# A recommendation tower on one core: the pair stage written out by chunk, moved by DMA, with paced gathers

## The chip, the cores and the metric

The kernel runs on one core of one Trainium2 chip. The metric is the device time of one execution in microseconds. A core has TensorE (PE: matmuls, with its weight loads shown apart as PEld), VectorE (DVE), ScalarE (ACT), GpSimd (POOL) and SyncE (SP), which run their own instruction streams in order and meet at semaphores. In a trace an fp32 matmul shows as two weight loads and two matmul records; a transpose shows as one of each. The documents below call one such weight load with its matmul a pass.

## The reference, cut to what matters

For 512 samples, 26 embedding rows of 64 numbers each are gathered from 26 tables. Then, with fixed weights:

```python
x = layer_norm(dense_t @ Wd.T, gd, bd)                       # 512 x 128
y = layer_norm(einsum('bnd,ed->bne', sparse_t, Ws), gs, bs)  # 26 rows of 128 per sample
y = layer_norm(einsum('bne,pn->bep', y, Wsi), gsi, bsi)      # 32 columns of 128 per sample
T = concatenate([x, y])                                      # 33 vectors of 128 per sample
Z = einsum('bnd,bmd->bnm', T, T)                             # all pair products
out = layer_norm(Z[lower triangle] @ Wl.T, gl, bl)[first 384 live]
h = relu(concatenate([out, dense]) @ W_top1 + b_top1)
h = relu(h @ W_top2 + b_top2);  y = h @ W_top3               # 512 x 1
```

## The kernel before, in words

The 512 samples are taken in NG = 4 granules of GRAN = 128, and a granule in NC = 4 chunks of 32 samples. A granule's 26 rows of 128 samples fill 13 tiles of two rows side by side (tile `G`), 4 tiles for chunk 0 and 3 for each other chunk. POOL gathers them with one indirect DMA for each tile and side: 8 for chunk 0, 6 for each other chunk, 26 a granule, 104 in all (L285). `G` holds one granule, so the gathers of a chunk wait until the chunk in the same place of the granule ahead was read by TensorE (`ut_ps`). Nothing else holds the gathers back.

One chunk goes through these steps. TensorE transposes the gathered tiles (`transpose_rows`, L941), multiplies them by a Gram matrix (`gram_rows`, L947), DVE turns that into a variance (`variance1`, L673, L677), ACT takes a root and DVE scales the rows (`scale_rows`, L683, L686). TensorE sums the fields into 32 columns a sample (`project_fields`, L958) and embeds them (`embed`, L968); DVE moves them to `V` (`y_evacuate`, L696), ACT squares them (`square2`, L381), DVE sums the squares (`variance2`, L701), ACT takes the root (L385), and DVE scales `V` (`normalise2`, L705, L707).

The pair products (`pair_products`, L990) run on half a granule, 64 samples: one matmul for each sample, weights 128x32 and 34 moving columns (32 of `V`, one of x, one of ones). Four samples stand beside one another in four column groups of 32. Of the symmetric products a ring of 16 columns is kept: `z_evacuate` (ACT, L390) copies the first 16 columns, `z_merge` (DVE, L748, L749) overwrites by a mask with the other 16. When a granule is done, `spread_pairs` (TensorE, L1002, L1008) brings them into blocks of 128 pairs by samples with 24 matmuls against pieces of the unit matrix, and ACT copies them to `zb` and `zx` (`z_copy`, L397, L398).

`project_pairs` (L1022) makes the 512 features of the granule, with features on partitions: 4 feature blocks by 5 pair blocks, 20 matmuls 128 columns wide. `f_squares` (L402), `sum_blocks3` (DVE, L712), `sum_squares` (TensorE, L1030), `deviation3` (ACT) and `normalise3` (DVE, L716, L718) normalise them. `layer1` (L1045), `layer2` (L1054), `layer3` (L1062) follow.

The order is written by hand for each engine. A granule's 4 slots are `slots01` and `slots23`; the work on pairs of a granule is spread over the slots of the granules behind it. Slots of the middle granules are in a hardware loop (`Fori(1, NG - 1)`, two passes) on ACT, DVE and TensorE (L552, L863, L1196); the first and last are written out. SP has the weight loads at the start, each behind the landing of a chunk of gathers of granule 0 (L258 to L266), and the one store at the end.

## Time and profile before

| what | value |
|---|---|
| time, median of 3 runs | 244.02 us (243.06 to 245.71) |
| profiled execution, its own time | 243.04 us |
| its span | 241.2 us, 4708 instructions |
| PE busy | 173.7 us (72%), 1983 passes |
| PEld busy | 131.6 us (55%) |
| DVE busy | 121.1 us (50%), 225 instructions |
| ACT busy | 76.2 us (32%) |
| POOL busy | 108.1 us (45%), 104.0 of it gathers |
| mean granted TensorE clock | 0.83 of full |
| "issue" on the chain of waits | 17% of the span |
| "another core or an unknown queue" on it | 13% |
| DMA traffic | 8.14 MB, mean 34 GB/s |

The span runs from the first to the last instruction; the execution's own time is 1.8 us more. Busy times are of one engine and overlap with those of others. "issue" is time in which an engine waited for nothing that the profile shows. "remote" stands where the profile knows no releaser. The two levels of the granted clock are 1.2 and 2.4 GHz; a fraction is a mean over them.

### The profile page before, as it was taken

How to read it: one execution, taken by the hardware profiler on the slowest of the kernel's cores; microseconds unless marked ns; L12 is line 12 of the kernel's file. 1: busy time of each engine (PE TensorE's matmuls, PEld its weight loads, DVE VectorE, ACT ScalarE, POOL GpSimd, SP SyncE). 2: the span in 40 equal slices, each digit the busy share in tenths (PEclk: the TensorE clock that was granted, in tenths of full speed). 3: DMA queues.
4: the chain of work that ended last, by engine and by line, in shares of the span. 5: the costliest groups of instructions: out<-in, count | busy, mean ns of one | idle time of the engine just before them, and what ended most of it. 6: DMA issues, size and time to landing. Idle time of an engine off the chain costs nothing.

```text
span 241.2 us, 4708 instructions
## 1 busy us (share of the span) xinstructions
PE 173.7 (72%) x1983; PEld 131.6 (55%) x1983; DVE 121.1 (50%) x225; ACT 76.2 (32%) x158; POOL 108.1 (45%) x110
## 2 busy tenths in 40 slices
PE   0668825649981954689558728979929799867896
PEld 0318721235551724458528518846729686767695
DVE  6474400238958270546482920916863984773012
ACT  2021400026684420515321310414414165350224
POOL 3787777727775173456570660557450000330000
PEclk9985555757996796899875955997967999999999
DMA  6515453101111010010110010011010000000000
GB/s 190 178 24 125 111 155 97 45 5 26 28 22 29 3 30 16 14 22 16 20 26 8 16 24 6 11 24 22 16 27 0 0 0 1 0 3 5 0 3 0
DMA packets 5728, 8.14 MB, mean 34 GB/s; under 512 B 2357, under 2 KB 3279, under 8 KB 5712
## 3 DMA queue, kind: packets, MB, share of 16 engines
q0 software_dynamic: 3328, 3.41, 7.4%
q1 hardware_dynamic: 1664, 3.65, 5.0%
q10 hardware_dynamic: 720, 0.85, 1.2%
q8 instruction: 12, 0.20, 0.4%
q14 instruction: 4, 0.03, 0.0%
HBM read 7.91 MB, written 0.00 MB: 33 GB/s over the span
## 4 chain that ended last, share of the span: by engine, by line
PE 53%; issue 17%; another core or an unknown queue 13%; DVE 9%; ACT 5%; DMA 2%; ACTq 1%; DVEq 0%
PE ps_z L990 8%; PE ps_gq L947 6%; PE ps_y L968 5%; PE ps_ut L958 5%; PE ps_tail L1045 4%; PE ps_tail L1022 3%; PE ps_z L1002 3%; PE ps_tail L899 2%; DVE var L701 2%; DMA gs_sb<-in_gs_row_dram 2%; PE ps_y L1022 2%; PE ps_gq L941 2%; PE ps_tail L931 2%; PE ps_tail L1054 1%
## 5 line engine op out<-in xcount | busy, mean ns | idle before, releaser
L285 POOL DMA_INDIRECT G<-in_table_dram,idx x104 | 104.0, 1000 | 74.9 <-PE ps_ut L958 41.7
L990 PE MATMUL ps_z<-V 128*32 128x34 f32 x1024 | 21.1, 218 | 28.0 <-issue 26.3
L673 DVE TENSOR_TENSOR qg<-ps_gq,G 128x384 f32<-128x384 f32 (+1 forms) x16 | 9.4, 588 | 57.0 <-PE ps_gq L947 23.2
L990 PEld LDWEIGHTS ps_z<-V 128*32 128x32 f32 x1024 | 16.9, 128 | 35.3 <-issue 32.3
L968 PE MATMUL ps_y<-ut,wcg 64*128 64x512 f32 x64 | 21.6, 751 | 7.2 <-issue 7.0
L958 PE MATMUL ps_ut<-S,G 128*128 128x192 f32 (+4 forms) x128 | 25.1, 348 | 2.2 <-DVE G L686 1.5
L947 PE MATMUL ps_gq<-gram,gt 128*128 128x128 f32 x104 | 19.2, 335 | 8.9 <-ACT gt L367 7.7
L958 PEld LDWEIGHTS ps_ut<-S,G 128*128 128x128 f32 x128 | 23.5, 229 | 3.2 <-DVE G L686 2.1
L701 DVE TENSOR_REDUCE var<-sq 128x32 f32<-128x1024 f32 x16 | 19.4, 1213 | 8.5 <-ACT sq L381 7.9
L381 ACT ACTIVATE sq<-V 128x1024 f32<-128x1024 f32 x16 | 16.9, 1058 | 20.3 <-DVE V L696 20.3
L947 PEld LDWEIGHTS ps_gq<-gram,gt 128*128 128x128 f32 x104 | 16.4, 236 | 10.5 <-ACT gt L367 7.8
L696 DVE TENSOR_TENSOR V<-ps_y,bias_y 128x512 f32<-128x512 f32 x32 | 20.6, 683 | 2.5 <-remote 2.5
L291 POOL TENSOR_TENSOR V<-V,r_pool 128x1024 f32<-128x1024 f32 x2 | 3.8, 1924 | 31.2 <-DVE r_pool L817 31.2
L707 DVE TENSOR_TENSOR V<-V,r 128x1024 f32<-128x1024 f32 x14 | 17.2, 1226 | 0.5
L367 ACT COPY gt<-ps_gq 128x384 f32<-128x384 f32 (+1 forms) x16 | 8.0, 502 | 29.1 <-PE ps_gq L941 23.7
L1022 PEld LDWEIGHTS ps_tail<-zb,wl 128*128 128x128 f32 x96 | 13.3, 214 | 3.9 <-issue 3.8
L1022 PE MATMUL ps_tail<-zb,wl 128*128 (+1 forms) x96 | 15.1, 307 | 0.0
L372 ACT ACTIVATE sd<-var,eps 128x6 f32<-128x6 f32 (+1 forms) x16 | 4.8, 300 | 29.1 <-DVE var L677 22.5
L941 PE MATMUL ps_gq<-eye,G 128*128 128x128 f32 x52 | 10.8, 332 | 3.6 <-issue 2.0
L376 ACT COPY ut<-ps_ut 128x512 f32<-128x512 f32 x16 | 9.4, 586 | 12.2 <-remote 8.0
L1045 PE MATMUL ps_tail<-zn,w1z 128*128 128x128 f32 x72 | 10.5, 308 | 2.5 <-DVE zn L718 1.2
L1045 PEld LDWEIGHTS ps_tail<-zn,w1z 128*128 128x128 f32 x72 | 9.9, 221 | 2.8 <-issue 2.6
(138 smaller groups left out, 228.3 us busy)
## 6 DMA issues: line engine op xcount, KB each, us to landing
G<-in_table_dram,idx POOLq DMA_INDIRECT x104
w1z<-in_w_z_dram SPq DMA_DIRECT2D x1, 768.0 KB
wl<-in_wl_blocks_dram SPq DMA_DIRECT2D x1, 768.0 KB
dns<-in_dense_t_dram ACTq DMA_DIRECT2D x1, 512.0 KB
w1d<-in_w_d_dram SPq DMA_DIRECT2D x1, 512.0 KB
wl<-in_wl_blocks_dram SPq DMA_DIRECT2D x1, 512.0 KB
w2s<-in_w_dram SPq DMA_DIRECT2D x1, 512.0 KB
wrow<-in_wsi_rows_dram SPq DMA_DIRECT2D x1, 208.0 KB
```

The lines of the kernel that those rows point to most:

```text
L285: pool.indirect_dma_start(G[:, j, g, :], None, table, bass.IndirectOffsetOnAxis(ap=idx[:, k:k + 1], axis=0)).then_inc(gathered[c], 16)
L381: act.activation(sq2[:, :, :], chunk_v(c), ACT.Square).then_inc(sq_ready, 1)
L696: dve.tensor_tensor(V[:, b0:b0 + CB, 0:NPROJ], ps_y[:, g, :].rearrange("p (b q) -> p b q", q=NPROJ), bias_y[:, :].unsqueeze(1).broadcast_t ...
L701: dve.reduce_sum(var2[:, :], sq2[:, :, :], AX_X).then_inc(var2_ready, 1)
L707: dve.tensor_tensor(chunk_v(c), chunk_v(c), r2[:, :].unsqueeze(2).broadcast_to([P, CHUNK, NPROJ]), ALU.mult).then_inc(v_ready, 1)
L941: mm = pe.transpose(ps_gq[:, n * P:(n + 1) * P], G[:, j, :, :].rearrange("p g d -> p (g d)"), eye[:, :])
L947: mm = pe.matmul(ps_gq[:, n * P:(n + 1) * P], gt[:, n * P:(n + 1) * P], gram[:, :], start=True, stop=True)
L958: mm = pe.matmul(ps_ut[:, chunk % 2, col:col + n], G[:, j, :, :].rearrange("p g d -> p (g d)"), S[:, j, :, :].rearrange("p s q -> p (s q)" ...
L968: pe.matmul(ps_y[:, g, :], wcg[64 * g:64 * g + 64, :], ut[64 * g:64 * g + 64, :], start=True, stop=True).then_inc(y_ps, 1)
L990: mm = pe.matmul(ps_z[32 * qb:32 * qb + 32, bb // 8, col:col + SLOTS], V[:, b, 0:NPROJ], V[:, b, :], start=True, stop=True)
L1022: mm = pe.matmul(bank[:, lc, :], wl[:, k, lc * P:(lc + 1) * P], rhs, start=(k == 0), stop=(k == KB - 1))
L1045: mm = pe.matmul(tail[:, oc, :], w1z[:, k, oc * P:(oc + 1) * P], zn[:, k, :], start=(k == 0), stop=(k == LLIVE - 1))
```

## The change

- **Gathers.** `G` holds all four granules. The wait for `ut_ps` is gone. Before the gathers of chunk n (n counts all 16 chunks) POOL waits until those of chunk n - 1 have landed. Each chunk has a semaphore of its own.
- **Pair products.** They run by chunk, 16 times, two samples a matmul: weights 128x64 (two samples' 32 columns), 67 moving columns (one of ones, two of x, 64 of `V`), two matmuls beside one another in two column groups of 64. 16 matmuls a chunk, 256 in all, for 512. Of each result the two samples' own blocks are used.
- **Evacuation.** `z_evacuate` is two ACT copies a chunk; `z_merge` two COPY_PREDICATED and two small copies on DVE a chunk. The places of the samples are permuted in the gathers' ids so that they come out in order.
- **Moves.** For granules 0 to 2 `spread_pairs` and `z_copy` go. SP issues 24 DMAs a granule from `zt` to `zb` and `zx`, 32 partitions each, rows of 128 bytes. Granule 3 keeps the matmuls (`last_spread`).
- **Projection.** For granules 0 to 2 samples are on partitions: 5 matmuls, 512 columns wide, for 20 of 128. The squares are summed by the accumulator of ACT's Square, root and scale are one number a partition (ACT does the scale), three transposes turn the features back (`transpose_features`), ACT copies them to `zn`. `sum_blocks3`, `sum_squares` and `normalise3` go.
- **Order.** All loops are written out. Slot n has `transpose_rows(n)`, `project_fields(n-1)`, `gram_rows(n)`, `embed(n-1)`, `pair_products(n-2)`, and the evacuation of chunk n-3. In the last granule POOL scales one chunk of `V`, for two before.
- **Start.** `prepare_b1`, `prepare_x` and the dense products are placed later or one by one through `ps_tail`.

```diff
-        G = sb("G", [P, TILES, 2, D])
+        G = sb("G", [P, NG, TILES, 2, D])
...
-            for gp in range(NG):
-                for c in range(NC):
-                    if gp:
-                        pool.wait_ge(ut_ps, nth(gp - 1, c))
-                    for j in batch(c):
-                        for g in range(2):
-                            k = gp * 2 * TILES + 2 * j + g
-                            pool.indirect_dma_start(
-                                G[:, j, g, :], None, table,
-                                bass.IndirectOffsetOnAxis(ap=idx[:, k:k + 1], axis=0)).then_inc(gathered[c], 16)
-            for n, c in enumerate(POOL_CHUNKS):
-                pool.wait_ge(r2_ready, nth(NG - 1, c))
-                pool.tensor_tensor(chunk_v(c), chunk_v(c), r2_pool[:, n, :].unsqueeze(2).broadcast_to([P, CHUNK, NPROJ]),
-                                   ALU.mult).then_inc(v_pool_ready, 1)
+            for n in range(NCHUNK):
+                if n > 0:
+                    pool.wait_ge(gathered[(n - 1) // NC][(n - 1) % NC], 2 * len(batch((n - 1) % NC)) * 16)
+                for j in batch(n % NC):
+                    for g in range(2):
+                        k = n // NC * 2 * TILES + 2 * j + g
+                        pool.indirect_dma_start(
+                            G[:, n // NC, j, g, :], None, table,
+                            bass.IndirectOffsetOnAxis(ap=idx[:, k:k + 1], axis=0)).then_inc(gathered[n // NC][n % NC], 16)
...
+            def move_pairs(gp):
+                sp.wait_ge(z_merged, (gp + 1) * NC)
+                for qb in range(4):
+                    src = zt[32 * qb:32 * qb + 32, gp % 2, :, qb % 2, :]
+                    at = slice(gp * GRAN + 32 * qb, gp * GRAN + 32 * qb + 32)
+                    for q in range(4):
+                        sp.dma_start(zb[32 * q:32 * q + 32, :, at], src[:, PQ * q:PQ * q + PQ, :]).then_inc(z_moved, 16)
+                    sp.dma_start(zx[ROW_XV:ROW_XV + 32, at], src[:, RING, :]).then_inc(z_moved, 16)
+                    sp.dma_start(zx[ROW_S:ROW_S + 32, at], src[:, RING + 1, :]).then_inc(z_moved, 16)
+            for gp in range(NG - 1):
+                move_pairs(gp)
...
+            def z_evacuate(n):
+                if n >= 2 * NC:
+                    act.wait_ge(z_moved, (n // NC - 1) * MOVES * 16)
+                act.wait_ge(z_ps, n + 1)
+                for w in range(2):
+                    last = act.copy(z_places(n, w), z_pairs(w)[:, :, :, 0:RING])
+                last.then_inc(z_first, 1)
...
+            def f_squares(gp):
+                act.activation(f_sq[:, :, :], tail, ACT.Square, accum_out=f_sum[:, :]).then_inc(f_sq_ready, 1)
+            def deviation3(gp):
+                act.wait_ge(f_sq_ready, gp + 1)
+                act.activation(sd3[:, 0:1], f_sum[:, :], ACT.Sqrt, bias=eps[:, :], scale=1.0 / L).then_inc(sd3_ready, 1)
+            def f_scale(gp):
+                act.wait_ge(r3_ready, gp + 1)
+                act.activation(f_scaled[:, :, :], tail[:, 0:LLIVE, :], ACT.Copy, scale=r3[:, 0:1]).then_inc(f_ready, 1)
+            def zn_copy(gp):
+                act.wait_ge(ft_ps, gp + 1)
+                act.copy(zn[:, :, :], tail[:, 0:LLIVE, :]).then_inc(zn_ready, 1)
...
+            def z_merge(n):
+                dve.wait_ge(z_first, n + 1)
+                for w in range(2):
+                    dve.copy_predicated(z_places(n, w), mmask[:, :].unsqueeze(1).unsqueeze(1).broadcast_to([P, 4, 2, RING]),
+                                        z_pairs(w)[:, :, :, RING:NPROJ])
+                x_at, s_at = (zt[:, n // NC % 2, m, :, n % NC * 8:n % NC * 8 + 8].rearrange("p l (w s) -> p w s l", w=2)
+                              for m in (RING, RING + 1))
+                dve.tensor_copy(x_at, z_slots[:, :, :, 1:3])
+                dve.tensor_copy(s_at, z_slots[:, :, :, 0:1].broadcast_to([P, 2, 4, 2])).then_inc(z_merged, 1)
...
+            def slot(n):
+                gp, c = divmod(n, NC)
+                normalise2(n - 2)
+                if n >= 3:
+                    z_merge(n - 3)
+                if c == 1 and gp > 1:
+                    add_dense(gp - 2)
+                variance1(n)
+                x_slots(n - 1)
+                scale_rows(n)
+                if n == 3:
+                    prepare_last_block()
+                if c == 3 and gp > 0:
+                    root3(gp - 1)
+                y_evacuate(n - 1)
+                variance2(n - 1)
...
-                for bb in range(16):
-                    for qb in range(4):
-                        b = h * HALF + 16 * qb + bb
-                        col = (bb % 8) * SLOTS
-                        mm = pe.matmul(ps_z[32 * qb:32 * qb + 32, bb // 8, col:col + SLOTS], V[:, b, 0:NPROJ],
-                                       V[:, b, :], start=True, stop=True)
+                    pe.wait_ge(z_merged, n)
+                for w in range(2):
+                    for s in range(4):
+                        for ct in range(2):
+                            v = n % NC * CB + 8 * w + 2 * s + ct
+                            mm = pe.matmul(ps_z[64 * ct:64 * ct + 64, w, s * SLOTS:(s + 1) * SLOTS], V[:, v, 3:SLOTS],
+                                           V[:, v, :], start=True, stop=True)
                 mm.then_inc(z_ps, 1)
...
+            def project_pairs(gp):
+                pe.wait_ge(wl_ready, 2)
+                pe.wait_ge(dense_ready, OC1)
+                if gp > 0:
+                    pe.wait_ge(yo_ready, gp)
+                pe.wait_ge(z_moved, (gp + 1) * MOVES * 16)
+                at = slice(gp * GRAN, (gp + 1) * GRAN)
+                for k in range(KB):
+                    mm = pe.matmul(ps_tail[:, :], zb[:, k, at] if k < PB else zx[:, at], wl[:, k, :],
+                                   start=(k == 0), stop=(k == KB - 1))
+                mm.then_inc(f_ps, 1)
...
+            def slot(n):
+                gp, c = divmod(n, NC)
+                transpose_rows(n)
+                project_fields(n - 1)
+                gram_rows(n)
+                if n == 3:
+                    prepare_dense(1)
+                if n == 4:
                     prepare_last_block()
+                if n == 5:
+                    prepare_dense(2)
+                if n == 6:
+                    prepare_dense(3)
+                if c == 3 and gp > 0:
+                    project_pairs(gp - 1)
+                if c == 0 and gp > 1:
+                    transpose_features(gp - 2)
+                if c == 1 and gp > 1:
+                    layer2(gp - 2)
+                embed(n - 1)
+                pair_products(n - 2)
+                if c == 0 and gp > 1:
+                    layer1(gp - 2)
+                if c == 1 and gp > 1:
+                    layer3(gp - 2)
...
+            gp, n = NG - 1, NCHUNK - 1
+            transpose_rows(n)
+            project_fields(n - 1)
+            gram_rows(n)
+            embed(n - 1)
+            pair_products(n - 2)
+            project_fields(n)
+            embed(n)
+            project_pairs(gp - 1)
+            pair_products(n - 1)
+            transpose_features(gp - 1)
+            pair_products(n)
+            layer1(gp - 1)
+            last_spread(gp)
+            layer2(gp - 1, ocs=range(1))
+            last_project_pairs(gp)
+            last_layer1(gp, range(1))
+            last_sum_squares(gp)
+            last_layer1(gp, range(1, OC1))
+            layer2(gp - 1, ocs=range(1, OC2))
+            last_layer2(gp)
+            layer3(gp - 1)
+            last_layer3(gp)
...
```

## Rows read from the trace of the kernel before

**Rows 1.** The longest waits of the whole span: engine, line, releaser, total, times, longest.
```profile
...
PE ps_z L990 <- issue: 26.3, 34, 1.8
...
```

**Rows 2.** The gathers, all shapes: busy, mean ns, idle before, releasers.
```profile
...
L285 POOL DMA_INDIRECT G<-in_table_dram,idx x104 | 104.0, 1000 | 74.9 <-PE ps_ut L958 41.7 <-issue 28.0 <-DVE idx L570 3.2
...
```

**Rows 3.** Stretches with gathers in flight, then one without: width, busy (records) by engine.
```profile
...
71.60:78.60 7.00, 1.21 (x12) 0.78 (x12) 4.87 (x8) 2.63 (x5) 3.95 (x5) 0.72 0.13 25
87.00:94.40 7.40, 1.59 (x20) 1.17 (x19) 2.05 (x5) 0.23 (x1) 4.69 (x5) 0.82 0.16 29
...
136.70:145.40 8.70, 2.53 (x26) 1.50 (x27) 3.36 (x7) 1.25 (x2) 5.73 (x6) 0.67 0.15 26
...
188.30:189.70 1.40, 1.32 (x129) 1.19 (x128) 1.36 (x3) 0.67 (x2) 0.00 (x0) 1.00 0.00 0
...
```

**Rows 4.** The same view, from a gather burst's start until the pair products stall.
```profile
...
118.81:123.50 4.69, 4.28 (x51) 2.72 (x51) 2.19 (x4) 1.28 (x4) 3.78 (x4) 0.64 0.13 24
134.02:136.70 2.68, 2.54 (x50) 1.36 (x48) 2.58 (x5) 1.21 (x4) 2.07 (x3) 1.00 0.07 12
172.12:174.50 2.38, 2.36 (x54) 1.37 (x53) 1.52 (x3) 0.68 (x3) 1.89 (x2) 1.00 0.07 14
...
```

**Rows 5.** Time line of POOL: start, length, operation, idle before.
```profile
...
21.93 0.95 POOL L285 DMA_INDIRECT G<-in_table_dram,idx  x1 [0.30 <-issue]
...
91.96 0.95 POOL L285 DMA_INDIRECT G<-in_table_dram,idx  x1 [0.30 <-issue]
...
118.81 0.95 POOL L285 DMA_INDIRECT G<-in_table_dram,idx  x1 [1.59 <-remote]
...
```

**Rows 6.** Time line of TensorE, four wide passes and the end of a stalled burst.
```profile
...
84.49 1.98 PE L915 MATMUL ps_tail<-dns,w1d 128*128 128x512 f32 x4
...
94.47 1.24 PE L990 MATMUL ps_z<-V 128*32 128x34 f32 x67 [0.49 <-issue]
...
```

**Rows 7.** Time line of SyncE's DMA issues.
```profile
...
16.86 0.33 SPq L259 DMA_DIRECT2D pmask<-in_pair_mask_dram  x1
...
17.70 0.43 SPq L261 DMA_DIRECT2D w1d<-in_w_d_dram  x1
24.27 8.18 SPq L264 DMA_DIRECT2D wl<-in_wl_blocks_dram  x2
...
```

**Rows 8.** DMA issues: size, median us from issue to landing.
```profile
...
wd<-in_wd_t_dram ACTq DMA_DIRECT2D x1, 128.0 KB, 2.3
...
```

**Rows 9.** Groups by line and shape, DVE and ACT: count, busy, mean ns.
```profile
...
L701 DVE TENSOR_REDUCE var<-sq 128x32 f32<-128x1024 f32 x16 | 19.4, 1213 | 8.5 <-ACT sq L381 7.9 <-issue 0.6
...
L707 DVE TENSOR_TENSOR V<-V,r 128x1024 f32<-128x1024 f32 x14 | 17.2, 1226 | 0.5
L381 ACT ACTIVATE sq<-V 128x1024 f32<-128x1024 f32 x16 | 16.9, 1058 | 20.3 <-DVE V L696 20.3
...
L673 DVE TENSOR_TENSOR qg<-ps_gq,G 128x384 f32<-128x384 f32 x12 | 6.6, 553 | 45.8 <-remote 19.5 <-PE ps_gq L947 19.2 <-issue 7.0
...
L705 DVE RECIPROCAL r<-sd 128x32 f32<-128x32 f32 x14 | 4.8, 344 | 0.4 <-ACT sd L385 0.4
...
L749 DVE COPY_PREDICATED zt<-mmask,ps_z 128x256 f32<-128x256 int32 x8 | 3.8, 470 | 0.0
...
L748 DVE COPY zt<-ps_z 128x32 f32<-128x32 f32 x8 | 1.5, 186 | 5.1 <-ACT zt L390 5.1
...
```

**Rows 10.** Time line of DVE, first chunks.
```profile
...
46.60 0.56 DVE L673 TENSOR_TENSOR qg<-ps_gq,G 128x384 f32<-128x384 f32 x1 [19.52 <-remote]
...
56.11 0.56 DVE L673 TENSOR_TENSOR qg<-ps_gq,G 128x384 f32<-128x384 f32 x1 [0.85 <-PE ps_gq L947]
...
```

**Rows 11.** Time line of DVE, last granule.
```profile
...
191.41 1.28 DVE L696 TENSOR_TENSOR V<-ps_y,bias_y 128x512 f32<-128x512 f32 x2
...
203.88 0.56 DVE L673 TENSOR_TENSOR qg<-ps_gq,G 128x384 f32<-128x384 f32 x1 [3.25 <-PE ps_gq L947]
...
```

**Rows 12.** Time line of ACT at the second pass of the loop.
```profile
...
161.80 0.59 ACT L397 COPY zb<-ps_z 128x512 f32 x1 [6.20 <-remote]
...
```

765 lines of the change are left out of this document (300 added, 465 removed).

## The prediction, made before the changed kernel ran

> **What bounds the kernel now.** I read the waits by total first. The longest of TensorE is on the pair products, with no releaser: 26.3 us in 34 pieces [rows 1]. Then I cut the span around those pieces. In three stretches of 7 to 9 us inside a burst of pair products only 12, 20 and 26 passes ran; in a stretch without the stall 129 ran in 1.40 us [rows 3]. All three lie where POOL issues gathers. One burst resumes at 94.47 [rows 6], 1.56 us after the last gather of its batch left POOL (91.96 + 0.95) [rows 5], and 1.4 us is what a gather takes to land: chunk 1's last one leaves POOL at 22.88 and SP, which waits for it, issues at 24.27 [rows 5, 7]. So the stall ends when no gather is in flight.
>
> The reader is to see a reserve that drains. From the start of a gather burst to the stall TensorE ran 51 passes in 4.7 us, 50 in 2.7 and 54 in 2.4 [rows 4]; in the stall it gets 58 passes in 23.1 us, 2.5 a us [rows 3]. 51 - 2.5 x 4.7 = 39, 50 - 7 = 43, 54 - 6 = 48. I read: TensorE has some 44 passes of instructions in hand, and while gathers fly it is supplied with about 2.5 a us. The trace shows the rates; that it is instruction supply is my inference.
>
> Three other stalls have no releaser: 19.52 us on DVE at the start, ending at 46.60 [rows 10], 6.20 us on ACT at the second pass of the loop [rows 12], and smaller ones. Gathers wait 41.7 us for TensorE [rows 2], but they run ahead and cost nothing by themselves.
>
> **The change, part by part.**
>
> *Gathers.* One takes 1.000 us and 0.30 between two (28.0 over 92) [rows 2], so 104 take 135. Each of 15 pauses costs the landing, 1.4 us, and about 0.1 of handing over: 22. From 3.7 on, the last leaves POOL at 161 and lands at 162.6. Chunks land every 9.2 us, 11.8 for chunk 0. No end of this kernel can be earlier than the last landing, some 3 us to its variance, and the tail.
>
> What a pause gives: after the one of 1.59 us at 118.81 [rows 5] TensorE again had a reserve of 39 [rows 4], though a burst of gathers had only just ended. So I let each pause refill it. Bounds: nothing, and 44 passes plus what runs meanwhile.
>
> *Pair products.* 64 passes a chunk become 32. Four abreast with 34 columns, a pass costs 1.32/129 = 10 ns [rows 3]; with 67 columns and two abreast it is four times that, 41 ns, so 1.3 us a chunk for 0.7. The lower bound is 0.35 us (the rate of before for 32 passes), the upper 32 x 0.5 us = 16 by the pass of 512 columns, far away and taken for nothing. It lies beside DVE.
>
> *Passes.* A slot now needs 53 (3 transposes, 6 Gram, 8 projection, 4 embedding, 32 pairs), chunk 0 three more; the wide projection adds 10 in slots 7 and 11, transposes and layer 1 27 in slots 8 and 12, layers 2 and 3 20 in slots 9 and 13, the start 28. From slot 2 to 14 this is 840.
>
> *DVE in a slot.* Reciprocal 0.34, scaling of V 1.23, variance 0.55 and 0.55, scaling of rows 0.55, sum of squares 1.21 [rows 9], two evacuations 1.28 [rows 11], x column and small reciprocal 0.4. The new z_merge: two COPY_PREDICATED of 128 elements, between half of 0.47 and all of it, I take 0.30 (the halves are strided in four dimensions), and two copies of 0.19 [rows 9]: 1.0, bounds 0.85 and 1.3. Sum 7.1. It waits for ACT's square, 1.06 and 0.1 [rows 9], and about 0.7 for the two roots: 9.0 us a slot. This is a closed chain, since slot n+1 begins with what slot n ends with, so it sets the pace where PE keeps up. ACT's extra copies are hidden in it. The f-path leaves DVE (reciprocal of 128, sum, scaling, 2.6 us a granule), which the 9.0 already leaves out.
>
> *Start.* DVE's stall up to 46.60 [rows 10] stays by my forecast: the same loads follow the same landings. `variance1(2)` then begins at about 56.1 as before [rows 10]. The later places of `prepare_b1` and `prepare_x` are hidden under this stall; without it they would cost under 2 us.
>
> *Moves.* For each granule 24 issues on SP, 0.42 us each (16.86 to 17.70 for two) [rows 7], 10.1, and 2.3 to land [rows 8]: 12.4 us. SP has nothing else queued; the store comes last. z_merge ends 2.6 us into slot n; the projection is wanted before `embed` in slot n+1, which DVE wants 5.0 us into that slot. So the moves are there 12.4 + 2.6 - 9.0 = 6.0 into it. Then come 10 wide passes (four took 1.98 [rows 6], so 4.6) and 1.1 of embedding: 11.7. DVE, and ACT's square behind it, wait 6.7 us, in slots 7 and 11: 13.4. In the last granule the projection stands behind the last `embed`, with 13 us to spare. Bounds of this term: 0 if the passes of the projection fall into a slot that is late anyway, 25 if issues of 128-byte rows take twice as long.
>
> The Trainium skill, DMA: Bandwidth & Descriptors, under "Anatomy of one DMA — SWDGE (gpsimd) path", gives about 2.0 us of fixed cost for a DMA, mostly its completion. As an estimate by that page the 15 pauses would cost 9 us more and the last landing be at 172, still ahead of DVE's pace; the row's 1.4 stands.
>
> *Loops written out.* The stalls at the loop's turn (6.20 on ACT [rows 12]) go. What they hid is next late: DVE's chain. The streams become longer; bounds 0 and one such stall a granule, 18 us.
>
> *Tail.* `variance1` of the last chunk begins at 203.88 [rows 11], 37.3 before the end of 241.2. The last burst is 32 passes, not 128, layer 1 has no reciprocal ahead of it: 35.0. One chunk of V more is scaled by DVE, in the shadow of PE.
>
> *Sum.* 56.1 + 13 slots x 9.0 = 173.1; dmat's eleven small operations 2.1; moves 13.4: 188.6. Supply: from 46.6 to 161.6 it gives 115 x 2.5 = 287 and the 44 in hand, and 44 for each of 11 pauses. By 161.6 slots 2 to 11 must be done, some 630 passes: 7 of 11 refills do, so no cost. 188.6 + 35.0 = 223.6 of span, 225.4 with the 1.8 around it, against 243.0 of the profiled execution. The median of the runs is 1.0 above that; I say 226.
>
> **Rivals.**
>
> *The supply stays starved: slower.* Place: TensorE, slots 2 to 14; price 44 passes, 18 us, for each pause that does not refill, beyond the spare ones. The moves are DMAs too and may fill pauses. To be no slower than before, `variance1(15)` must begin by 207; then slots up to 9 must be done at 161.6, 515 passes: fewer than 5 refills of 11 make it slower. With 4, 331 + 176 passes reach the end of slot 9; 5.1 slots and one wait for moves follow, 161.6 + 46 + 7 + 35 + 1.8 = 251; with none 272. For it: in all bursts the stall begins within a few us. Against it: the pause at 118.81.
>
> The Trainium skill, Runtime: NRT & Kernel Launch, "Instruction fetch mechanics", says that fetch is hidden by the rate of issue and only a taken branch breaks it. By that rule this rival has no ground, and the 26 us would have another cause; the rows at the loop's turn agree with its second half, the stall in unbranched bursts speaks against its first. I give the rival 17 in 100.
>
> *The start-up stall goes, the moves are hidden: the gathers bound.* 162.6 + 3 + 35.0 + 1.8 = 202. For it: the pauses open the same gap for DVE that they open for TensorE. Against: the weight loads are the same bytes. 20 in 100.
>
> *Longer streams stall by themselves.* One stall of 6.2 a granule for three granules, 18 us on top of 226: 244, no change. For it: DVE's 19.52 us is in code without a branch. 11 in 100.
>
> **How the numbers follow.** My case has 52 in 100, by itself 212 to 240 (moves 0 to 25 with 14 taken, z_merge +-3, a wait or two for supply). What a measurement of this kernel can tell from no change is about 1%, 241.6 to 246.5. Slower by over 1%: the starved rival and a little of the stalls, 0.19. Within 1%: most of the third rival's 11, less what lies to its sides, 0.07. Faster: the rest, 0.74. The range is 202 to 246: it holds my case, the gather bound and the third rival, and leaves out the starved one.
>
> **What would show it.** POOL's gathers in 16 groups with about 1.6 us between, the last near 161. Pair bursts of 32 passes without gaps of over a us beside gathers; gaps of 0.7 and 1.2 us there prove the starved rival. DVE's `variance1` every 9 us, with 6 to 7 more in slots 7 and 11, where TensorE waits for the moves. A DVE start near 46; near 32 it is the second rival. I am wrong if DVE idles for long on PE in other slots, if the pause does not refill, or if the moves take far over 12 us.

## The result

The changed kernel takes 264.42 us (median of 4 runs, 259.58 to 266.46), the kernel before 244.87 beside it (243.06 to 246.26): ratio 1.068, interval [1.050, 1.087]. It is slower by 20 us; the forecast was 226. Ratios here and below leave out runs over 1.5% above the fastest of their kernel (here two of the four), so they can differ from those of the medians shown. The profiled execution took 265.47 us, its span is 263.7.

| what | value after |
|---|---|
| PE busy | 176.8 us, 1234 passes |
| PEld, DVE, ACT busy | 124.2, 136.5, 79.8 us |
| POOL busy | 108.7 us |
| mean granted clock | 0.81 |
| on the chain of waits | PE 30%, DVE 20%, issue 14%, ACT 13%, SP's queue 11% |

749 passes fewer, and PE is as busy as before. The longest waits of the kernel after (columns: engine, line, what it waited for, total us, times, longest); the first answers to [rows 1]:

```profile
PE ps_gq L892 <- ACT gt L372: 29.1, 12, 4.6
ACT sq L386 <- DVE V L693: 29.1, 15, 6.8
...
POOL G L290 <- DMA G<-in_table_dram,idx: 24.6, 14, 1.9
...
PE ps_tail L947 <- DMA zx<-zt: 16.3, 3, 8.8
```

TensorE's wait without a releaser on the pair products is no longer among PE's long ones. In its place PE waits for ACT's copy of the transposes, and for the moves. DVE in the kernel after, around its third `variance1` and in one bare slot (start, us, engine, line, operation, what ended the idle time before it); the first line answers to [rows 10], the others to [rows 9]:

```profile
31.48 0.56 DVE L666 TENSOR_TENSOR qg<-ps_gq,G 128x384 f32<-128x384 f32 x1 [5.93 <-issue]
...
45.00 0.56 DVE L666 TENSOR_TENSOR qg<-ps_gq,G 128x384 f32<-128x384 f32 x1 [0.46 <-PE ps_gq L892]
```

```profile
158.71 1.27 DVE L718 COPY_PREDICATED zt<-mmask,ps_z 128x128 f32<-128x128 int32 x2
159.60 0.40 DVE L722 COPY zt<-ps_z 128x16 f32<-128x16 f32 x1
159.67 0.36 DVE L723 COPY zt<-ps_z 128x16 f32<-128x16 f32 x1
159.74 0.67 DVE L666 TENSOR_TENSOR qg<-ps_gq,G 128x384 f32<-128x384 f32 x1
...
162.07 1.28 DVE L693 TENSOR_TENSOR V<-ps_y,bias_y 128x512 f32<-128x512 f32 x2
164.47 1.22 DVE L700 TENSOR_REDUCE var<-sq 128x32 f32<-128x1024 f32 x1 [1.12 <-ACT sq L386]
166.08 0.35 DVE L704 RECIPROCAL r<-sd 128x32 f32<-128x32 f32 x1 [0.39 <-ACT sd L390]
...
168.64 0.67 DVE L666 TENSOR_TENSOR qg<-ps_gq,G 128x384 f32<-128x384 f32 x1
```

The start is 11 us earlier than I took it, since DVE's stall of 19.5 us did not come back (5.9 at 31.48). A slot runs here from one `variance1` to the next, and a bare one is one without preparation, projection or layers; it takes 168.64 - 159.74 = 8.9 us, as worked out. But few are bare. `variance1` begins, for chunks 2 to 15, at 45.00, 58.50, 71.19, 86.84, 98.96, 111.27, 133.80, 149.20, 159.74, 168.64, 192.14, 202.19, 214.38 and 223.28: 13 slots take 178.3 us, for 132.5 forecast.

The moves and the projection of granule 1, on SP's queue and on PE, and the last gather and a pause on POOL, answer to [rows 7, 6, 5]:

```profile
160.06 2.58 SPq L268 DMA_DIRECT2D zb<-zt  x4
162.67 0.61 SPq L269 DMA_DIRECT2D zx<-zt  x1
...
175.00 0.59 SPq L270 DMA_DIRECT2D zx<-zt  x1
```

```profile
176.91 6.64 PE L947 MATMUL ps_tail<-wl,zb 128*128 128x512 f32 x8 [8.80 <-DMA zx<-zt]
183.38 1.02 PE L947 MATMUL ps_tail<-wl,zx 128*128 128x512 f32 x2
184.34 1.13 PE L914 MATMUL ps_y<-ut,wcg 64*128 64x512 f32 x4
```

```profile
17.89 0.94 POOL L290 DMA_INDIRECT G<-in_table_dram,idx  x1 [1.73 <-DMA G<-in_table_dram,idx]
...
162.41 0.95 POOL L290 DMA_INDIRECT G<-in_table_dram,idx  x1 [0.30 <-issue]
```

24 issues take 175.59 - 160.06 = 15.5 us, 0.65 each, and the last has landed 1.3 us after its end. PE waits 8.80 us for them, and then the ten wide passes take 7.4 us, ahead of `embed`. Their granted clock, PE having been idle for 8.8 us, is 0.58 over 177 to 184, mostly the level of 1.2 GHz:

```profile
177.00:184.00 7.00, 7.00 (x10) 2.76 (x10) 0.00 (x0) 0.00 (x0) 0.00 (x0) 0.58 0.00 0
```

(Columns: stretch, length, busy us and number of instructions of PE, PEld, DVE, ACT and POOL, granted clock, DMA share, GB/s.)

In one longer stretch PE does starve, in the pair products of chunk 6 and layer 1 behind them:

```profile
131.78 0.84 PE L933 MATMUL ps_z<-V 128*64 128x67 f32 x21
...
133.78 0.32 PE L933 MATMUL ps_z<-V 128*64 128x67 f32 x3 [0.50 <-issue]
...
136.65 0.49 PE L933 MATMUL ps_z<-V 128*64 128x67 f32 x3 [0.97 <-ACT zn L415]
137.39 4.68 PE L962 MATMUL ps_tail<-zn,w1z 128*128 128x128 f32 x20 [0.25 <-issue]
```

### The profile page after: what moved, and what is told of

It is laid out like the page before. It is cut to its first block, busy times and chain, and to the rows that moved or that the text cites. A ratio compares the mean times of both kernels' runs of the same rounds, so it can differ in the third digit from the quotient of the medians.

```text
span 263.7 us, 3259 instructions
## 1 busy us (share of the span) xinstructions
PE 176.8 (67%) x1234; PEld 124.2 (47%) x1234; DVE 136.5 (52%) x277; ACT 79.8 (30%) x182; POOL 108.7 (41%) x109
## 4 chain that ended last, share of the span: by engine, by line
PE 30%; DVE 20%; issue 14%; ACT 13%; SPq 11%; POOL 5%; DMA 3%; another core or an unknown queue 3%; DVEq 0%
SPq L268 7%; POOL G L290 5%; PE ps_tail L947 5%; DVE V L693 4%; ACT sq L386 4%; DVE var L700 4%; PE ps_tail L962 3%; DVE zt L718 3%; PE ps_y L914 3%; PE ps_tail L971 3%; DVE V L706 3%; PE ps_gq L892 2%; PE ps_ut L904 2%; PE ps_tail L876 2%
## 5 line engine op out<-in xcount | busy, mean ns | idle before, releaser
L290 POOL DMA_INDIRECT G<-in_table_dram,idx x104 | 106.5, 1024 | 56.4 <-issue 28.5
L892 PE MATMUL ps_gq<-gram,gt 128*128 128x128 f32 x104 | 23.4, 387 | 34.8 <-ACT gt L372 29.1
L892 PEld LDWEIGHTS ps_gq<-gram,gt 128*128 128x128 f32 x104 | 19.7, 279 | 37.8 <-ACT gt L372 30.3
L296 POOL TENSOR_TENSOR V<-V,r_pool 128x1024 f32<-128x1024 f32 x1 | 1.9, 1912 | 66.2 <-DVE r_pool L712 66.2
L718 DVE COPY_PREDICATED zt<-mmask,ps_z 128x128 f32<-128x128 int32 x32 | 20.4, 824 | 16.8 <-ACT zt L398 16.8
L700 DVE TENSOR_REDUCE var<-sq 128x32 f32<-128x1024 f32 x16 | 19.5, 1219 | 16.1 <-ACT sq L386 11.7
L933 PEld LDWEIGHTS ps_z<-V 128*64 128x64 f32 x512 | 18.6, 147 | 18.7 <-issue 18.7
L947 PE MATMUL ps_tail<-wl,zb 128*128 128x512 f32 x24 | 16.3, 841 | 16.3 <-DMA zx<-zt 16.3
L933 PE MATMUL ps_z<-V 128*64 128x67 f32 x512 | 21.9, 237 | 5.7 <-DVE zt L723 2.6
L947 PEld LDWEIGHTS ps_tail<-wl,zb 128*128 128x128 f32 x24 | 6.3, 275 | 25.0 <-issue 25.0
L666 DVE TENSOR_TENSOR qg<-ps_gq,G 128x384 f32<-128x384 f32 (+1 forms) x16 | 10.1, 631 | 13.5 <-issue 9.9
L727 DVE RECIPROCAL r<-sd 128x1 f32<-128x1 f32 x3 | 0.5, 164 | 29.5 <-ACT sd L407 18.3
L962 PE MATMUL ps_tail<-zn,w1z 128*128 128x128 f32 x72 | 12.1, 335 | 2.4 <-issue 1.6
```

The lines of the kernel that those rows point to most:

```text
L290: pool.indirect_dma_start(G[:, n // NC, j, g, :], None, table, bass.IndirectOffsetOnAxis(ap=idx[:, k:k + 1], axis=0)).then_inc(gathered[n ...
L700: dve.reduce_sum(var2[:, :], sq2[:, :, :], AX_X).then_inc(var2_ready, 1)
L718: dve.copy_predicated(z_places(n, w), mmask[:, :].unsqueeze(1).unsqueeze(1).broadcast_to([P, 4, 2, RING]), z_pairs(w)[:, :, :, RING:NPROJ])
L892: mm = pe.matmul(ps_gq[:, i * P:(i + 1) * P], gt[:, i * P:(i + 1) * P], gram[:, :], start=True, stop=True)
L933: mm = pe.matmul(ps_z[64 * ct:64 * ct + 64, w, s * SLOTS:(s + 1) * SLOTS], V[:, v, 3:SLOTS], V[:, v, :], start=True, stop=True)
L947: mm = pe.matmul(ps_tail[:, :], zb[:, k, at] if k < PB else zx[:, at], wl[:, k, :], start=(k == 0), stop=(k == KB - 1))
```

## The experiments

**They ran in six sets, and the sets were of two kinds.** Every set carries runs of the kernel before. In the sets of e1 to e4, e9 to e12 and e17 to e18 it took 188.5, 187.8 and 188.3 us; in those of e5 to e8, e13 to e14 and e15 to e16 it took 243.3, 243.3 and 244.8, as in the result. I call them quiet and starved sets. One chip number had a starved set and, later, a quiet one, so it is not a property of the number. Runs are compared within a kind alone.

*The kernel before, unchanged, in a starved and in a quiet set.*

> The kernel before, unchanged. Beside the last four kernels it took 188.5 us, not 244. What makes the difference of 55 us is open. Theory of the supply: the stalls without a releaser are another amount in these runs; the 26.3 us on TensorE's pair products, the 19.5 us on DVE at the start and the 6.2 us on ACT at the loop's turn are below 5 together, and what is left is busy time and the gathers, which then end near 141 (104 x 1.30 + 3.7). Rival, the engines or the transfers themselves were slower then: the mean durations of a gather, of a matmul pass and of DVE's operations are lower here by a like share.

> The kernel before, unchanged, for its profile beside the next three. It took 188 us beside the first four kernels and 243 beside the second four, where the stalls without a releaser were as in the profile shown. If it takes 188 here: no stall without a releaser over 2 us on any engine, the last gather out near 141, the last variance1 near 150, a tail of 37: bound by the gathers. If it takes 243: the stalls are there, and all of them lie before the last gather has landed.

Measured: 241.01 and 187.58 us. Waits in the starved one (e5), then in the quiet one (e9), and the chain of waits of e9 by engine:

```profile
PE ps_z L990 <- issue: 23.4, 43, 1.2
...
DVE qg L673 <- issue: 16.7, 1, 16.7
ACT sd L372 <- issue: 15.5, 5, 8.3
```

```profile
PE ps_z L990 <- issue: 2.2, 2, 1.3
```

```profile
PE 150.8 (81%) x1983; PEld 115.4 (62%) x1983; DVE 120.7 (65%) x225; ACT 75.8 (41%) x158; POOL 111.0 (60%) x110
...
POOL 50%; PE 22%; issue 16%; DVE 7%; ACT 2%; DMA 1%
```

DVE has no such wait in e9 and ACT one of 2.1 us, and PE's on the pair products falls from 23.4 to 2.2. All waits with "issue" or "remote" behind them come to 31, 28 and 50 us on PE, DVE and ACT in e5, and to 3, 0 and 2 in e9. A gather's mean on POOL is 1.03 us in both, and the gathers' packets took 7.4% of 239.2 us in e5 and 10.2% of 185.7 in e9, so the transfers are not quicker. Without the stalls the kernel before is bound by its gathers: the last leaves POOL at 141.06, `variance1` of the last chunk begins at 148.69, and the end is 37.0 later, as expected. What differs from set to set is the waits for nothing that the profile shows; I call them stalls of supply, without knowing what is supplied. With what follows from them they are worth 239.2 - 185.7 = 53.5 us to the kernel before. For the rival (slower engines) speaks only PE: its mean granted clock is 0.84 against 0.95 and its busy time 174.2 us against 150.8. How much of the 53.5 goes through the clock is not separated. DVE's busy time is the same, 121.2 and 120.7 us.

**The traces of the two kinds also differ in how complete they are.** A gather's landing should leave 16 records of a semaphore, 104 x 16 = 1664 in all, as in e1 and e10. The ten traces of quiet sets have 1634 to 1664 of them, the ten of starved sets 262 to 857 (`before` 545, `after` 761, e14 below 262); and their pages give no time from issue to landing for the gathers, where the quiet ones give 2.5 us. Two things follow. In a starved trace the named releasers are uncertain, and an "issue" or "remote" can hide an ordinary wait. And a rival stands that no run tests: that writing the profiler's own records is what holds the engines back in these sets. Every run on record has a span and a clock, so none shows the time without such records.

*The changed kernel, unchanged, in either kind.*

> The changed kernel, unchanged, beside the same runs of the kernel before as the experiments. Late projection took 225.3 us there and the changed kernel without the moves 231.8. Theory of the moves: this is 12 to 15 us above the late projection, 237 to 241, a ratio of 1.26 to 1.28. Rival, the late projection gains nothing: 224 to 228. Variance1 every 9 us, save slots 7 and 11 of 20 to 23 us.

> The changed kernel, unchanged. Theory of two costs: its own chain (slots of 10 to 11 us of DVE, ACT and TensorE by turns, and the moves) makes some 238 us wherever there are no stalls of supply, and the stalls add 25. So if the kernel before takes 188 beside it, this takes 236 to 241; if the kernel before takes 243, this takes 262 to 266. Rival, its time is all supply: then it is below 225 where the kernel before takes 188.

Measured: 263.38 us in the starved set, ratio 1.086 [1.078, 1.095]; 250.99 in the quiet one, ratio 1.337 [1.329, 1.345]. e6's expectation (237 to 241) was meant for the quiet kind and is 10 below even that, as is e10's (236 to 241). So the stalls cost the changed kernel 11 us of span (261.3 - 250.1), not 53.5: **starved sets cost it much less, and in a quiet set its own chain is 64 us longer** (250.1 - 185.7). That is not to say that the stalls are gone. The waits with "issue" or "remote" are 11, 22 and 32 us on PE, DVE and ACT in e6, for 31, 28 and 50 in e5 and 1, 0 and 2 in e10. On PE two thirds went; on DVE and ACT most stayed, and the longer slots have room for them. How much was removed and how much is only hidden is not separated.

PE, ACT and DVE in slot 9 of e10, where layer 2 of granule 0 stands ahead of `embed`:

```profile
132.40 3.75 PE L971 MATMUL ps_tail<-h,w2s 128*128 128x128 f32 x16 [2.86 <-ACT h L419]
136.09 2.08 PE L914 MATMUL ps_y<-ut,wcg 64*128 64x512 f32 x4
```

```profile
131.63 0.63 ACT L419 ACTIVATE h<-h_pre 128x512 f32<-128x512 f32 x1 [2.12 <-DVE h_pre L731]
...
136.19 0.62 ACT L424 ACTIVATE h<-ps_tail,sm 128x128 f32<-128x128 f32 x2 [3.22 <-PE ps_tail L971]
139.52 1.06 ACT L386 ACTIVATE sq<-V 128x1024 f32<-128x1024 f32 x1 [2.70 <-DVE V L693]
```

```profile
131.51 0.54 DVE L666 TENSOR_TENSOR qg<-ps_gq,G 128x384 f32<-128x384 f32 x1
...
138.20 1.29 DVE L693 TENSOR_TENSOR V<-ps_y,bias_y 128x512 f32<-128x512 f32 x2 [4.40 <-PE ps_y L914]
...
144.80 0.67 DVE L666 TENSOR_TENSOR qg<-ps_gq,G 128x384 f32<-128x384 f32 x1
```

DVE wants `embed` at 133.8 and waits 4.40 us: PE has waited 2.86 for `relu1` (ACT, behind `add_dense` on DVE) and then runs 16 passes. ACT's `square2` in turn stands behind `relu2`. The slot takes 13.3 us for 8.9. The starts of `variance1` in e10 give the sum: bare slots (10, 14) 8.9; with transposes and layer 1 (8, 12) 10.1 each; with layers 2 and 3 (9, 13) 13.3 each; with parts of the preparation (2 to 6) 10.9, 12.8, 14.0, 9.8, 13.3; with the projection and the moves (7, 11) 18.3 and 22.4. Together 166.1 us.

*Without the moves; and the projection a slot later.*

```diff
-            for gp in range(NG - 1):            # e1, with the waits on z_moved
-                move_pairs(gp)
...
-                if c == 3 and gp > 0:           # e2, and all that follows it too
-                    project_pairs(gp - 1)
+                if c == 0 and gp > 1:
+                    project_pairs(gp - 2)
```

> The changed kernel without the 72 transfers on SP that move z to the projection's rows, and without what waits for them; the projection starts when z_merge is done and reads zeros, so the moved values are left out of the computation. Theory of the moves: in the changed kernel 24 issues take 16.3 us, TensorE waits 5.5 and 8.8 us for them in slots 7 and 11 and 2.0 in the tail, and ACT and DVE stand behind it. Without them slots 7 and 11 still hold the ten wide passes (6.8 us each), so they take some 16 us instead of 22.5 and 23.5, and the time is 16 to 20 us lower: 245 to 249. Rival, the moves are beside the path and the slots are long by the wide passes and by instruction supply: not more than 4 us lower, 260 to 264. Second rival, the transfers also feed the pauses of the supply: then the stall at 131 to 144 us (slot 8, 15.4 us) goes too, and it is 25 lower, below 240.

> The changed kernel with the projection of granules 0 to 2 and all that follows it one slot later, so that the moves have 9 us more. Theory of the moves: TensorE's waits for the transfers (5.5 and 8.8 us) go, the ten wide passes stay, so 12 to 15 us lower: 249 to 252. The tail's granule 2 is one slot later as well, which could give 2 to 5 of it back. Rival, the wide passes at 1.2 GHz and the work behind them are what costs, wherever they stand: within 3 us of the changed kernel.

Measured, both in a quiet set: 231.77 us (231.62 to 233.76) and 225.3 (225.17 to 228.92), ratios to the kernel before 1.236 [1.226, 1.246] and 1.198 [1.187, 1.209]. The expected levels started from the starved 264 and don't apply to a quiet set; against its 250.99 the moves are worth 19 us, in the 16 to 20 expected, and the late projection 26, more than the 12 to 15. With no moves slots 7 and 11 still take 14.1 and 13.5 us, since the wide passes stay in line:

```profile
148.11 5.64 PE L932 MATMUL ps_tail<-wl,zb 128*128 128x512 f32 x8
153.59 1.02 PE L932 MATMUL ps_tail<-wl,zx 128*128 128x512 f32 x2
```

The late projection keeps all passes and all moves and is the faster of the two, so it is where the projection and what follows it stand, not PE's total work, that costs. The rival of e2 (within 3 us) fails. It is still 37 us slower than the kernel before.

*The moves undone; the late projection with ACT's copies in another order.*

```diff
+                if c == 2 and gp > 0:           # e7: matmul spread and ACT copies in slot c == 2
+                    last_spread(gp - 1)
+                    pe.wait_ge(z_sb, gp)
...
-                gt_copy(n)                      # e8: with e2's edit
-                z_evacuate(n - 3)
...
+                gt_copy(n + 1)
+                z_evacuate(n - 2)
                 deviation2(n - 1)
```

> The changed kernel with the moves alone undone: 24 matmuls against slices of the identity and two copies on ACT in the third slot after the granule, as the kernel before has them. Theory of the moves: SP's 16.3 us of issues per granule go, 24 passes of TensorE (about 6 us at half clock) and 1.5 us of ACT come into one slot: 12 to 20 us below the changed kernel of the same call, some 222 to 228. Rival, it is the passes of TensorE that bound: equal or slower than the changed kernel.

> The late projection, and in ACT's order the copy of the next chunk's transposes and the evacuation of z ahead of the second deviation of the chunk before. Theory of ACT's order: TensorE's Gram passes wait 29.8 us for that copy though the transposes were done long before; the copy gets 3 to 5 us earlier in each of 12 slots where DVE's chain does not need it first, so DVE's variance1 follows its other work at once: 2 us a slot, 200 to 215. Rival, the copy is off the path: the wait of TensorE moves elsewhere, within 3 us of the late projection alone (225).

Measured, in a starved set: 245.08 us (242.25 to 256.72), ratio 0.999 [0.989, 1.009], and 243.17 (235.20 to 254.38), ratio 0.969 [0.960, 0.979]. Against 263.38 in the same set the spread by matmul gains 18 us, in the middle of the 12 to 20 expected; its absolute level was again forecast for a quiet set. e8 has no partner without ACT's order in its set, so what that order gives by itself is not shown: the 2 us a slot expected are not to be seen, since a bare slot of its profiled run (168.96 to 177.87) is 8.9 as well. Its four runs took 235.20, 235.65, 250.70 and 254.38 us, too far apart to settle what the kernel is worth.

*Pauses off in the changed kernel, on in the kernel before.*

```diff
-                if n > 0:                       # e3, e11, e17
-                    pool.wait_ge(gathered[(n - 1) // NC][(n - 1) % NC], ...)
...
+                    if gp or c:                 # e4, e12, e16 (e18: if c % 2 == 1)
+                        pgp, pc = divmod(gp * NC + c - 1, NC)
+                        pool.wait_ge(gathered[pc], (pgp + 1) * 2 * len(batch(pc)) * 16)
```

> The changed kernel without POOL's wait for the landing of the previous chunk. Theory of the supply (TensorE gets about 2.5 passes a us while gathers fly, a pause refills 44): the gathers end some 22 us earlier, near 141, and up to there TensorE gets 44 + 2.5 x 95 passes, about 280, where the slots of the changed kernel up to 141 hold some 500. The 220 that are missing come after 141: pair bursts show gaps of 0.4 to 1.2 us with no releaser through slots 2 to 8, and the time is 10 to 40 us higher, 275 to 300. Rival, pauses do nothing for the supply: the time is the same or up to 5 us lower and the pair bursts run without gaps.

> The kernel before with the one part of the change alone that a chunk's gathers wait for the landing of those of the chunk ahead. Theory of the supply: the wait of TensorE with no releaser on the pair products (26.3 us) shrinks below 10, because each pause refills some 44 passes; chunk periods of 64 pair passes need 85 a chunk, so a part of it stays. The gathers end near 163 or later. Time 230 to 242. Rival, the pauses only delay the gathers and the stall is of another kind: 26 us of it stay and the time is 245 to 260.

> The changed kernel without POOL's wait for the landing of the previous chunk, again beside other kernels. Where the kernel before takes 188: 248.5 was measured, and the changed kernel 236 to 241 beside it would say that the pauses help even there, by 8 to 12 us; equal times would say that pauses are neither here nor there. Where the kernel before takes 243, theory of the supply: with no pauses to refill it, 15 to 40 us slower than the changed kernel, 278 to 303. Rival, the stalls last as long as gathers fly, so gathers that end 20 us earlier (near 141) end the stalls earlier: 5 to 15 us faster than the changed kernel, 249 to 258.

> The kernel before with the pauses alone, again beside other kernels. Where the kernel before takes 188, 212.8 was measured, 24 more, the length of 15 pauses: the gathers set its end. Where the kernel before takes 243, theory of refilling pauses: the stall on the pair products (26 us) shrinks below 10 and the time is 220 to 240. Rival, the stalls stay as long as gathers fly and the gathers end later: 250 to 265.

> The kernel before with the pauses alone. Where the kernel before takes 188: 213, for the third time. Where it takes 243, theory of refilling pauses: the stalls without a releaser go down and the time with them, to 220 to 240. Rival, the pauses (22 us) cost as much as they give: 241 to 262.

> The changed kernel without its pauses, for the third time. Where the kernel before takes 188: 249, as the changed kernel itself. Where the kernel before takes 243: the reordered kernel went from 250 to 340 without the pauses, with one gap of 50 us on TensorE. Theory of the supply, the same here: over 300, TensorE nearly idle until the last gather has landed near 140, then some 13 slots of 9 to 13 us and the tail. Rival, it was something of the new order: not above 275.

> The kernel before with a pause ahead of every second chunk only, 8 in place of 15. Where it takes 188: the pauses cost 1.6 us each on the path of the gathers: 25 x 8/15 = 13 more, 201. Where it takes 243: if each pause gives the same refill, half of the 14 us that 15 pauses gave: 237; if half the pauses suffice for the stalls and cost half the time, 225 or less.

| kernel | quiet set | starved set |
|---|---|---|
| changed | 250.99 (e10) | 263.38 (e6) |
| changed, no pauses | 248.55, 249.46, 249.02 (e3, e11, e17) | not run |
| before | 188.5, 187.8, 188.3 | 243.3, 243.3, 244.8 |
| before, 8 pauses | 199.99 (e18), ratio 1.064 [1.050, 1.078] | not run |
| before, 15 pauses | 212.82, 212.92 (e4, e12), ratio 1.132 [1.122, 1.142] | 230.55 (e16) |

In quiet sets a pause is pure cost where the gathers bound (12 us for 8, 25 for 15, so 1.5 to 1.7 each) and costs 2 us in all, within the spread of the runs, in the changed kernel, whose slots are longer than the gathers'. In the starved set the same 15 pauses gain 14 us (225.73 to 233.08 against 243.33 to 246.31 of the kernel before; there is no interval for it). PE's stall on the pair products is 13.1 us for 23.4 in e5:

```profile
PE ps_z L993 <- issue: 13.1, 24, 1.2
```

The forecast of below 10 for it was too good; the times of e12, e16, e17 and e18 came as expected, while e3's and e4's expectations were made for a starved set. e3, e11 and e17 fell into quiet sets, so the changed kernel without pauses was never seen starved; the next pair shows the effect in a sibling.

*The work in another order, with and without pauses, and then without the moves.*

```diff
-                transpose_rows(n)               # e13, TensorE's slot
-                project_fields(n - 1)
-                gram_rows(n)
-                if c == 3 and gp > 0:
-                    project_pairs(gp - 1)       # so the other extras
...
                 embed(n - 1)
+                project_fields(n)
+                transpose_rows(n + 1)
+                gram_rows(n + 1)
                 pair_products(n - 2)
+                if c == 3 and gp > 0:
+                    project_pairs(gp - 1)
...
                 y_evacuate(n - 1)               # DVE: z_merge beside ACT's square
+                z_merge(n - 3)
                 variance2(n - 1)
...
-            def move_pairs(gp):                  # e15 alone: spread by matmul, as e7
```

> The changed kernel with its work unchanged in amount but in another order. TensorE does the embedding of chunk n-1 first, then fields, transposes and Gram of n and n+1, then the pair products; the preparation, the projection and the layers of an earlier granule come last in a slot, and their ACT parts fill the gap before square2. DVE does z_merge while ACT squares. Theory of steps in line (slots with layer 2, the projection or a part of the preparation take 13 to 22 us where a bare one takes 8.9, because embed and square2 stand behind them): slots of 8 to 10 us throughout, and with the gathers paced the chunks land every 10.2 us, so 13 slots take 133, 29 to 41 less than in the changed kernel. Beside a kernel before of 188: 215 to 225. Beside 243: 225 to 240. Rival, the moves (16 us of issues on SP) hold the projection wherever it stands: slots of 13 and more remain at 7 and 11, 10 us less gain. Second rival, TensorE's own work bounds (8.6 us a slot at the clock of the bare slots): no more than 10 us gained.

> The same order without POOL's wait for the landing of the previous chunk. Where the kernel before takes 188: the pauses are on the path here as they were in the kernel before (25 us there), since the slots are shorter than the 10.2 us at which paced chunks land: 190 to 200, 15 to 25 below the paced one. Where the kernel before takes 243: theory of refilling pauses, the stalls without a releaser grow and eat the gain, equal or slower than the paced one; rival, stalls end with the gathers and these end 20 us earlier, 5 to 15 faster.

> The reordered kernel, paced, with the 72 transfers on SP replaced by the 24 matmuls a granule against slices of the identity that the last granule has anyway (1.1 us there) and two copies on ACT. In the reordered kernel TensorE waited 1.5 us and more for the moves in the slots of the projection, one such slot took 16.4 us where others took 8.1, and in the tail 6.8 us. Theory of the moves: slot 11 and the tail lose 6 to 8 us each, slot 7 some 3: where the kernel before takes 243, 230 to 236, the first version of the new form faster than the kernel before; where it takes 188, 205 to 220. Rival, the ten wide passes fill the same time: no more than 5 us below the reordered kernel (245 to 250).

Measured, all three in starved sets: 250.19 us (249.32 to 251.03), ratio 1.036 [1.026, 1.046]; **339.73** (333.98 to 342.25), ratio 1.409 [1.391, 1.426]; 248.32 (238.20 to 249.30) beside a kernel before of 244.82. Of these e13 was expected at 225 to 240. The windows of e14 while gathers fly and just behind them, and of e11 (the changed kernel without pauses, quiet set), with the columns given above:

```profile
30.00:60.00 30.00, 9.40 (x36) 7.64 (x36) 2.89 (x7) 0.30 (x1) 22.68 (x25) 0.50 0.27 70
60.00:90.00 30.00, 0.05 (x1) 0.05 (x1) 4.25 (x6) 3.59 (x6) 22.68 (x25) 0.50 0.15 27
90.00:120.00 30.00, 5.47 (x12) 1.89 (x12) 0.00 (x0) 0.59 (x1) 22.69 (x24) 0.50 0.15 26
...
140.00:170.00 30.00, 14.99 (x99) 10.71 (x98) 17.08 (x41) 11.48 (x28) 0.00 (x0) 0.83 0.00 1
```

```profile
30.00:60.00 30.00, 22.13 (x153) 14.06 (x153) 20.88 (x47) 11.63 (x24) 22.68 (x25) 0.89 0.28 71
60.00:90.00 30.00, 21.64 (x133) 13.79 (x134) 19.88 (x41) 13.94 (x33) 22.69 (x25) 0.80 0.16 28
90.00:120.00 30.00, 18.65 (x117) 10.44 (x116) 11.50 (x21) 10.08 (x21) 22.99 (x24) 0.75 0.22 35
```

```profile
89.95 1.65 PE L891 MATMUL ps_gq<-gram,gt 128*128 128x128 f32 x6 [50.55 <-issue]
...
111.06 2.08 PE L913 MATMUL ps_y<-ut,wcg 64*128 64x512 f32 x4 [17.66 <-issue]
...
148.21 0.27 PE L932 MATMUL ps_z<-V 128*64 128x67 f32 x1 [3.23 <-issue]
```

```profile
89.42 0.48 ACT L369 COPY gt<-ps_gq 128x384 f32<-128x384 f32 x1 [5.96 <-remote]
110.42 0.59 ACT L378 COPY ut<-ps_ut 128x512 f32<-128x512 f32 x1 [20.52 <-remote]
```

```profile
74.09 0.69 DVE L692 TENSOR_TENSOR V<-ps_y,bias_y 128x512 f32<-128x512 f32 x1 [40.69 <-remote]
...
127.22 0.56 DVE L665 TENSOR_TENSOR qg<-ps_gq,G 128x384 f32<-128x384 f32 x1 [42.12 <-remote]
```

In 90 us PE gets 48 passes, DVE 13 instructions, ACT 8, while POOL issues gathers at its full pace; in e11 PE gets 402 in the same 90 us. TensorE's gap of 50.55 us is not a stall of its own, though the profile calls it "issue". `gram_rows` waits for ACT's `gt_copy`, which ends at 89.90, 0.05 us before PE goes on; so it is at 111.06, where `embed` waits for `ut_copy` (111.01). The stalls with nothing owed are on DVE and ACT: `y_evacuate` starts at 74.09 on products that PE had done by 36.49, `ut_copy` at 110.42 on a result of 39.40, `variance1` at 127.22 on one of 91.60.

The last gather leaves at 135.01 + 0.95. The gaps do not end with it: inside one burst of pair products PE has gaps of up to 3.23 us until 150.3, some 13 us after that gather can have landed. From 154 on most chunks take 8 to 11 us. With pauses (e13) the same order has no wait with "issue" or "remote" of over 6.6 us on PE, DVE or ACT. e14's expectation said equal or slower by the theory, and 90 us slower is far more than the 10 to 40 that e3's gave for taking the pauses out. e14 was not run in a quiet set, so that its order alone, without pauses, is slow anywhere is not excluded by a run of its own; e3, e11 and e17 exclude it for the order of the changed kernel.

Do the engines wait for instructions? By the profile's view of DMA by window, the instruction queues moved 2 packets between 30 and 120 us in e14 and 6 in e11, and none between 85.5 and 135 us in e14. ACT went on at 110.42 and DVE at 127.22 all the same, so those two stalls did not end with a load of instructions.

In e13 the slots with transposes and layer 1 shrank to 8.5 and 8.1 us (180.18 to 188.26), but the expected 8 to 10 throughout did not come: up to the last gather the slots took 8.5 to 14.5, and the one with the moves behind it 16.4. The tail holds two lines of the moves' price, in e13:

```profile
213.03 6.44 PE L949 MATMUL ps_tail<-wl,zb 128*128 128x512 f32 x8 [6.76 <-DMA zx<-zt]
...
230.16 0.52 PE L994 MATMUL ps_z<-zt,eye 128*32 128x128 f32 x10
```

TensorE waits 6.76 us for the 24 transfers of granule 2; the 24 matmuls that do the same for granule 3 begin at 230.16 and are over 1.3 us later. e15 has no moves and one of its runs reached 238.2, the other three lie at 248 to 249: a gain over e13 is not shown, and 230 to 236 was wrong. The slots of its profiled run, one of the three, take 11 to 18 us from chunk 7 to chunk 11.

**A version that beats both** in a starved set is the kernel before with the pauses alone: 230.55 us, 14 less than the kernel before beside it and 34 less than the result of the change. All its four runs are below all seven of the kernel before. e8 was below it as well in two of its four runs (235), and above in the others. In quiet sets nothing beat the kernel before (188).

## Why the prediction was wrong, by its steps

- **Start.** Forecast: DVE's stall up to 46.6 stays, `variance1(2)` at 56.1. It began at 45.0: 11 us in favour. That stall belongs to the starved sets too: in e9 it is not there at all, and `variance1(2)` begins at 35.30. Whether the pauses or the later preparation shortened it here was not shown.
- **Supply.** Forecast: the pauses and the halved passes remove the stall at no cost. The size came near: the stalls cost the changed kernel 11 us of span where they cost the kernel before 53. That a pause helps in a starved set stands by e13 against e14 and by e16. The mechanism does not stand: I counted PE's passes alone, and in e14 it is DVE and ACT that stall, with PE behind them; I let a stall end with the last gather in flight, and there gaps go on 13 us longer. A reserve of 44 passes and 2.5 a us were not tested, and for instructions as the thing supplied the loads on the instruction queues give no support. How much of the gain is the pauses, how much the halved passes and how much the room in longer slots was not shown.
- **Slots of 9.0.** Right where bare (8.9, z_merge 1.3 for 1.0, its upper bound), and **this is the step that failed**: I let one bare slot stand for all 13 and added 2.1 for dmat and 13.4 for the moves. The prediction's own list of passes had 27 more in slots 8 and 12 and 20 more in 9 and 13, but priced them nowhere: I took them for work beside DVE. The transposes and layer 2 stand in line ahead of `embed`, with a round trip to ACT or DVE, and so do parts of the preparation: in slot 4 of e10 ten wide passes for the last block take 6.55 us of PE ahead of `embed`, and DVE waits 4.69 us. In e10 the extras come to 1.1 a slot for transposes and layer 1, 4.3 for layers 2 and 3, and 15.8 for five slots with parts of the preparation: 26.6 us against the 2.1 I had, 24.5 missing.
- **Moves.** The term of 13.4 measured 22.7 in e10 (18.3 + 22.4 - 18.0). An issue took 0.65 us, not 0.42. The landing came 1.3 us after the end of the last issue, 1.9 after its start, which is how the 2.3 was measured. That makes 16.8 a granule for 12.4. And the ten wide passes cost 6.5 us (e1) to 7.4, not 4.6. The four of 1.98 in [rows 6] ran at a granted clock of 1.00 and give 4.95 for ten, so the 4.6 was also a slip; those of granule 2 took 4.5 at 1.00 (231.97 to 236.50), those in e1 6.5 at 0.68, those of granule 1 7.4 at 0.58. In all 9.3 are missing. Bounds 0 to 25 held it.
- **Tail.** 35.0 forecast, 40.4 measured (41.7 in e10). I gave the projection 13 us to spare there; it has none. The moves of granule 2 end late (PE waits 1.97 for them, up to 231.97), and 4.5 us of wide passes stand ahead of the pair products of chunk 14.
- **Sum.** 223.6 - 11.1 (start) + 45.8 (slots) + 5.4 (tail) = 263.7, the span. Of the 45.8, 33.6 are there in the quiet set (24.5 + 9.3, rounding aside); the other 12 come in the starved set only, and the stretch at 131.78 above is part of them.
- **Rivals.** The time fell into the starved rival's range of 251 to 272, but not by its mechanism: with hardly a stall it is 251. No rival of mine had the chain of f steps in line, and that was the rival to have. I had given the slower side 19 in 100, nearly all of it for the starved rival.

The Trainium skill, Runtime: NRT & Kernel Launch, "Instruction fetch mechanics", says that the rate of issue hides the fetch of instructions and that a taken branch breaks it. In the quiet sets the traces agree (2.2 us on PE's pair products). The starved ones do not decide it: e14 has no loop, and DVE and ACT stall there for up to 38 us with their inputs done, but no load of instructions ended the stalls at 110.42 and 127.22. My reading, that instructions are withheld, stays unproven, and these two stalls speak against it.

## What to carry to other kernels

Price every slot of a pipeline with its extras in the engine's own order: a step with a round trip to another engine, placed ahead of the step that the next engine wants, costs its whole length, however idle the engine is on average. When the profile shows waits without a releaser on several engines at once, ask what the same kernel takes without them before planning around it: here it was 188 us for 243, and the two kinds of set called for opposite choices about pauses. Look also whether the trace is whole (here 262 to 857 of 1664 landing records in the starved sets), and read from the program what an engine waits for before calling its gap a stall. Twenty-four small transfers from one queue, at 0.65 us each, are dear against 24 small matmuls that take 1.3 us.
